# Two expert stages of an audio tower: a bias product over 128 rows, the row copy on ScalarE, products set further apart

## The reference

```python
# first mixture, 8 experts, hidden size 256
h = jax.nn.silu(jnp.einsum('td,edh->eth', xt, w1)) * jnp.einsum('td,edh->eth', xt, w3)
y = jnp.einsum('eth,ehd->etd', h, w2)
out = jnp.einsum('te,etd->td', comb, y) + shared
...
# second mixture, 10 experts, hidden size 512
h = jnp.einsum('nd,edh->enh', x2, e_w1) + e_b1[:, None, :]
h = jax.nn.elu(h)
eo = jnp.einsum('enh,ehd->end', h, e_w2) + e_b2[:, None, :]
y = jnp.einsum('end,ne->nd', eo, gates).reshape(B, T, d)
```

## Time and profile before

| | us |
|---|---|
| median of three runs | 1716.76 |
| lowest and highest | 1712.75, 1718.33 |
| span of the profiled execution | 1722.4 |
| PE busy in that span | 1464.1 (85%) |
| DVE busy | 995.0 (58%) |
| POOL busy | 683.3 (40%) |
| ACT busy | 570.8 (33%) |

### The profile page before, as it was taken

One profiled execution on the slowest core, in us unless ns is written; L12 is line 12 of the kernel. 1 busy time (PEld: TensorE's weight loads), 2 busy tenths in 40 slices (PEclk: granted clock), 3 DMA queues, 4 the chain that ended last, 5 costly groups with the idle time before them and its releaser, 6 DMA issues.

```text
span 1722.4 us, 31035 instructions
## 1 busy us (share of the span) xinstructions
PE 1464.1 (85%) x9288; PEld 1261.0 (73%) x9289; DVE 995.0 (58%) x3333; ACT 570.8 (33%) x1362; POOL 683.3 (40%) x1039
## 2 busy tenths in 40 slices
PE   6679577868888479898999889989999878999985
PEld 3465455648888458687888779877888877999963
DVE  4496776554444565366444744376342627999956
ACT  2434526121222130241134401542033324555524
POOL 0124455345777531225222350235212614556532
PEclk9798798989999776788798969988797989999997
DMA  5003100026777500100010011000000234666634
GB/s 174 1 19 98 19 24 29 20 81 176 219 217 221 171 1 1 37 1 21 17 37 2 1 37 37 1 2 19 19 1 1 78 97 128 176 183 174 182 113 144
DMA packets 102193, 128.32 MB, mean 75 GB/s; under 512 B 21015, under 2 KB 61181, under 8 KB 101842
## 3 DMA queue, kind: packets, MB, share of 16 engines
q1 hardware_dynamic: 88786, 102.36, 20.6%
q0 software_dynamic: 13312, 24.74, 4.4%
HBM read 96.13 MB, written 34.94 MB: 76 GB/s over the span
## 4 chain that ended last, share of the span: by engine, by line
PE 56%; DVE 17%; issue 10%; another core or an unknown queue 5%; DVEq 3%; ACT 3%; POOL 3%; DMA 1%; POOLq 0%; SPq 0%; ACTq 0%
PE psum L970 9%; PE psum L1113 8%; PE psum L979 7%; PE psum L1059 5%; PE psum L962 3%; DVE work L1500 3%; PE psum L1038 3%; PE psum L787 2%; PE psum L1122 2%; PE psum L1008 2%; PE psum L1081 2%; DVE stats L1483 2%; PE psum L1171 2%; PE psum L1092 1%
## 5 line engine op out<-in xcount | busy, mean ns | idle before, releaser
L1113 PE MATMUL psum<-NT,wreg 128*128 128x182 f32 (+1 forms) x1536 | 290.7, 350 | 7.2 <-ACT conv_rows L1401 6.9
L1113 PEld LDWEIGHTS psum<-NT,wreg 128*128 128x128 f32 x1536 | 276.0, 210 | 11.6 <-ACT conv_rows L1401 7.5
L2111 POOL DMA_INDIRECT rows_out<-work,expert_row_kept x208 | 206.2, 991 | 140.1 <-DVE work L1804 115.8
L970 PE MATMUL psum<-work 128*128 128x128 f32 x1664 | 224.2, 278 | 20.2 <-DVE work L1804 18.6
L970 PEld LDWEIGHTS psum<-work 128*128 128x128 f32 x1664 | 208.4, 196 | 27.2 <-issue 16.2
L1309 ACT ACTIVATE work<-psum,work 128x128 f32<-128x128 f32 x416 | 118.3, 368 | 108.7 <-PE psum L970 108.7
L2060 POOL TENSOR_TENSOR rstd<-var_eps,pack 128x6 f32<-128x6 f32 x40 | 56.6, 1417 | 243.2 <-DVE var_eps L1490 243.0
L787 PE MATMUL psum<-pack,work 128*128 128x128 f32 (+1 forms) x336 | 59.8, 335 | 84.1 <-DVE work L1500 74.6
L1831 DVE TENSOR_SCALAR work<-psum,expert_row_kept 128x128 f32<-128x128 f32 x208 | 72.8, 350 | 99.9 <-PE psum L962 42.0
L1822 DVE SCALAR_TENSOR_TENSOR work<-psum,work 128x128 f32<-128x128 f32 x416 | 117.1, 344 | 7.7
L787 PEld LDWEIGHTS psum<-pack,work 128*128 128x128 f32 (+1 forms) x336 | 49.6, 176 | 93.9 <-DVE work L1500 58.7
(11 more groups left out here) (339 smaller groups left out, 2937.6 us busy)
## 6 DMA issues: line engine op xcount, KB each, us to landing
work<-w_and_b SPq DMA_DIRECT2D x104, 258.0 KB
work<-in_ew SPq DMA_DIRECT2D x104, 256.0 KB
work<-rows_in SPq DMA_DIRECT2D x208, 65.0 KB
work<-rows_out SPq DMA_DIRECT2D x32, 384.0 KB, 3.8
rows_out<-work,expert_row_kept POOLq DMA_INDIRECT x208
work<-in_xT SPq DMA_DIRECT2D x8, 375.0 KB, 4.4
w_and_b<-in_ew SPq DMA_DIRECT2D x1, 2560.0 KB
out<-H SPq DMA_DIRECT2D x8, 320.0 KB
```

Of the source, the lines that this page charges most:

```text
L970: r_ = mm(v.ps1[:, c * P:(c + 1) * P], v.w1[:, c * P:(c + 1) * P], v.xT, start=True, stop=True)
L1113: r = mm(bank[:, half * HALF_PAIRS:half * HALF_PAIRS + p1 - p0], weights[:, m * P:(m + 1) * P], product_input(name, g, k, p0, p1), start=( ...
L2111: G.indirect_dma_start(rows_out[m], bass.IndirectOffsetOnAxis(ap=v.dest, axis=0), v.y, None, bounds_check=last, oob_is_err=False).then_inc ...
```

## The change

It has five parts, all in the two expert stages:

1. `ones3` and `rows3` get 128 rows, of which 125 are zero, so that the bias product has 128 rows of weights. DVE sets both to zero at the start of the program.
2. In `experts1` the copy of the transposed rows moves from DVE to ACT, ahead of `exp`. In `experts0` it stays on DVE.
3. `AHEAD` grows: transposition and copy 5 turns ahead (3 before), up-products and `silu`/`exp` 3 (2), `u` 2 (1). `keep` goes from 3 to 2. PE's order in a turn becomes `up`, `xT`, `down`.
4. PSUM banks: up-products 0 to 3, transposition 4 and 5, `down` 6 and 7. `down` of a tile therefore waits for `y` of two tiles before. Semaphores count by tile of the ring (8) instead of by u mod 4.
5. `keep` runs once for two tiles: it waits for both stores of the round before, and copies 4 columns. In `experts0` SP loads the weights anew once `up` has read them (before: once `u` was done).

```diff
-AHEAD = {"xT": 3, "up": 2, "silu": 2, "exp": 2, "u": 1, "down": 0, "y": 0, "keep": 3, "store": 0}
+AHEAD = {"xT": 5, "up": 3, "silu": 3, "exp": 3, "u": 2, "down": 0, "y": 0, "keep": 2, "store": 0}
...
-        ones3 = sb("ones3", [3, P], BF16)
+        ones3 = sb("ones3", [P, P], BF16)
...
-        rows3 = sb("rows3", [3, E1 * P], BF16)
+        rows3 = sb("rows3", [P, E1 * P], BF16)
...
-            v.ps1 = psum[:, 2 * (u % SLOTS), :]
-            v.psx = psum[:, 2 * (u % SLOTS), 0:P]
-            v.psy = psum[:, 2 * (u % SLOTS) + 1, 0:P]
+            v.ps1 = psum[:, u % SLOTS, :]
+            v.psx = psum[:, SLOTS + u % 2, 0:P]
+            v.psy = psum[:, SLOTS + 2 + u % 2, 0:P]
...
-                        sp.wait_ge(pool_done[k], pool.at(phase, "keep", k, r - GROUPS))
+                        sp.wait_ge(pool_done[u // 2], pool.at(phase, "keep", u // 2, i - 1))
                         load_row(u)
-                        sp.wait_ge(dve_done[k], dve.at(phase, "u", k, r - GROUPS))
+                        if m == 0:
+                            sp.wait_ge(pe_done[u], pe.at(phase, "up", u, i - 1))
+                        else:
+                            sp.wait_ge(dve_done[u], dve.at(phase, "u", u, i - 1))
                         load_w1(u)
...
                     e.wait_ge(dve_done[k], dve.at(phase, "u", k, r))
-
+                    if u >= 2:
+                        e.wait_ge(dve_done[u - 2], dve.at(phase, "y", u - 2, i))
+                    else:
+                        e.wait_ge(dve_done[u - 2 + RING], dve.at(phase, "y", u - 2 + RING, i - 1))
...
-                turns(e, [("xT", xT), ("up", up), ("down", down)], begin)
+                turns(e, [("up", up), ("xT", xT), ("down", down)], begin)
...
-                turns(e, [("silu", silu) if m == 0 else ("exp", exp)])
+                def xT(u, i):
+                    v = slots[u]
+                    k, r = u, i
+                    e.wait_ge(pe_done[k], pe.at(phase, "xT", k, r))
+                    nc.scalar.copy(v.xT, v.psx).then_inc(act_done[k], act.step(phase, "xT", k))
+
+                turns(e, [("silu", silu)] if m == 0 else [("xT", xT), ("exp", exp)])
...
-            V.memset(ones3[:], 1.0)
+            V.memset(ones3[:], 0.0)
+            V.memset(rows3[:], 0.0)
+            e.drain()
+            V.memset(ones3[0:3, :], 1.0)
...
-                turns(e, [("xT", xT), ("u", gated if m == 0 else elu), ("y", y)])
+                turns(e, [("xT", xT), ("u", gated), ("y", y)] if m == 0 else [("u", elu), ("y", y)])
...
-                    e.wait_ge(row_stored[u], i * 16 + m * 16 * RITERS)
+                    if u % 2:
+                        return
+                    for x in (u, u + 1):
+                        e.wait_ge(row_stored[x], i * 16 + m * 16 * RITERS)
```

More of the change, by code:

```diff
@@ L93, in run @@
             f(t % RING, i + t // RING)
-    for u in range(-3, 0):
+    for u in range(-FIRST_AHEAD, 0):
         run(0, u, first=True)
@@ L479, in audio_tower @@
         for u, v in enumerate(slots):
-            v.ps1 = psum[:, 2 * (u % SLOTS), :]
-            v.psx = psum[:, 2 * (u % SLOTS), 0:P]
-            v.psy = psum[:, 2 * (u % SLOTS) + 1, 0:P]
+            v.ps1 = psum[:, u % SLOTS, :]
+            v.psx = psum[:, SLOTS + u % 2, 0:P]
+            v.psy = psum[:, SLOTS + 2 + u % 2, 0:P]
         def chunk_steps(names):
             return [f"{n}{c}" for c in range(TILES) for n in names]
-        pe_done = [sem(f"pe_done{k}") for k in range(4)]
+        pe_done = [sem(f"pe_done{k}") for k in range(RING)]
         pe = Steps({
@@ L492, in audio_tower @@
             "shared0": (ITERS, LANES, ["up0_0", "up0_1", "up1_0", "up1_1", "down"]),
-            "experts0": (EITERS, SLOTS, ["xT", "up", "down"]),
+            "experts0": (RITERS, RING, ["xT", "up", "down"]),
             "attention": (ITERS, LANES, ["norm5T", "q0", "q1", "k0", "k1", "v"]
                           + chunk_steps(["sc", "cx"]) + ["oT", "out", "norm6T", "rc1", "scores"]),
-            "experts1": (EITERS, SLOTS, ["xT", "up", "down"]),
+            "experts1": (RITERS, RING, ["xT", "up", "down"]),
             "output": (OUT_ITERS, OUT_LANES, ["z"]),
         })
-        act_done = [sem(f"act_done{k}") for k in range(4)]
+        act_done = [sem(f"act_done{k}") for k in range(RING)]
         act = Steps({
@@ L503, in audio_tower @@
             "shared0": (ITERS, LANES, ["s0_0", "s0_1", "s1_0", "s1_1"]),
-            "experts0": (EITERS, SLOTS, ["silu"]),
+            "experts0": (RITERS, RING, ["silu"]),
             "attention": (ITERS, LANES, ["n5T", "q0", "q1", "k0", "k1", "v"] + chunk_steps(["kt"])
                           + ["oT", "n6T", "rc1", "kept"]),
-            "experts1": (EITERS, SLOTS, ["exp"]),
+            "experts1": (RITERS, RING, ["xT", "exp"]),
             "output": (OUT_ITERS, OUT_LANES, ["norm7"]),
         })
-        dve_done = [sem(f"dve_done{k}") for k in range(4)]
+        dve_done = [sem(f"dve_done{k}") for k in range(RING)]
         dve = Steps({
@@ L524, in audio_tower @@
             "mix_b": (ITERS, (2, 3), ["rstd4"]),
-            "experts0": (EITERS, SLOTS, ["keep"]),
+            "experts0": (RITERS, RING // 2, ["keep"]),
             "attention": (ITERS, LANES, ["rstd5", "b_out", "b_v", "rstd6", "turned"]),
-            "experts1": (EITERS, SLOTS, ["keep"]),
+            "experts1": (RITERS, RING // 2, ["keep"]),
             "output": (OUT_ITERS, OUT_LANES, ["rstd7"]),
@@ L965, in up @@
                     v = slots[u]
[L966 removed]
+                    k, r = u, i
                     e.wait_ge(w1_in[u], i * 16 + (16 + m * 16 * RITERS))
[L968 removed]
+                    if m == 0:
+                        e.wait_ge(dve_done[k], dve.at(phase, "xT", k, r))
+                    else:
+                        e.wait_ge(act_done[k], act.at(phase, "xT", k, r))
                     for c in range(4):
@@ L1826, in y @@
                     v = slots[u]
-                    k, r = slot_round(u, i)
+                    k, r = u, i
                     e.wait_ge(pe_done[k], pe.at(phase, "down", k, r))
                     e.wait_ge(row_stored[u], 16 * i + 16 * RITERS * m)
-                    e.wait_ge(pool_done[k], pool.at(phase, "keep", k, r))
+                    e.wait_ge(pool_done[u // 2], pool.at(phase, "keep", u // 2, i))
                     V.tensor_scalar(v.y, v.psy, v.gate, None, ALU.mult).then_inc(dve_done[k], dve.step(phase, "y", k))
-                turns(e, [("xT", xT), ("u", gated if m == 0 else elu), ("y", y)])
+                turns(e, [("xT", xT), ("u", gated), ("y", y)] if m == 0 else [("u", elu), ("y", y)])
             expert_tiles(0, "experts0")
@@ L2098, in keep @@
                     v = slots[u]
-                    k, r = slot_round(u, i)
-                    e.wait_ge(row_stored[u], i * 16 + m * 16 * RITERS)
+                    if u % 2:
+                        return
+                    for x in (u, u + 1):
+                        e.wait_ge(row_stored[x], i * 16 + m * 16 * RITERS)
                     e.reg_add(last, none, OUT_ROWS - 1)
-                    e.wait_ge(pe_done[k], pe.at(phase, "xT", k, r))
+                    e.wait_ge(pe_done[u + 1], pe.at(phase, "xT", u + 1, i))
                     G.tensor_tensor(keep_seen[:, u:u + 1], w("nought"), w("nought"), ALU.add)
-                    G.tensor_copy(v.kept[:], v.row[:, P:ROW]).then_inc(pool_done[k], pool.step(phase, "keep", k))
+                    pair = work[:, E_AT + u * ROW:E_AT + (u + 2) * ROW].rearrange("p (x c) -> p x c", c=ROW)
+                    G.tensor_copy(kept[:, u:u + 2, :], pair[:, :, P:ROW]
+                                  ).then_inc(pool_done[u // 2], pool.step(phase, "keep", u // 2))
                 def store(u, i):
                     v = slots[u]
-                    k, r = slot_round(u, i)
+                    k, r = u, i
                     e.wait_ge(dve_done[k], dve.at(phase, "y", k, r))
```

35 lines of the change are left out of this document (15 added, 20 removed).

## The result

The changed kernel takes 1713.58 us in the median of 20 runs (1702.02 to 1725.42), the kernel before, run beside it, 1724.65 (1712.04 to 1748.87). The ratio is 0.9943, with a 95% interval of 0.992 to 0.9966: 11 us gained, where 42 were forecast. The profiled execution took 1709.04 us.

The account below looks back on a forecast made before the run. PE was taken to bound the second stage (2.20 per tile, DVE close behind), PE plus waits for late signals the first. From the median 1716.8, 20 and 23 us off and 1 added gave 1675 us, range 1662 to 1698.

Parts of the forecast that it names:

- Second stage: Second expert stage: padding the bias product and moving the row copy to ACT cut 2.20 to 2.01 per tile, gaining 20 us.
- the bias product's load without idle time: Sign expected in the second stage's next profile: no idle time at the padded bias product's weight load, before .12 us.
- that rival: Second stage: the bias product keeps its price, which comes from changing between f32 and bf16; 1695 us, chance .12.
- VectorE's bound: Second stage: DVE needs 2.15 us per tile, close behind PE's 2.20, so a faster PE alone wins .06 at best.
- First stage: First expert stage: larger distances and own banks add .60 of slack against late signals, gaining 23 us (bounds 0 and 31).
- The 22 waits of .97: First stage: PE's waits of `up` for DVE's row copy, 21 us in all, fall to at most .37 each, 8 us.
- the other 10 of the 31 us: First stage: the remaining waiting of PE is short pieces that the .60 of added slack covers.
- Late signals stay in full measure: Rival, first stage: more slack lets POOL run on longer, holds grow, gain 4 us or less; 1694 us, chance .15.
- POOL stays at 1.42 against 1.45: First stage, point for the late-signals rival: POOL's work per tile stays just under PE's turn, leaving almost no pause.
- POOL's backlog shrinks: First stage, point against the late-signals rival: with `keep` paired, POOL needs 1.42 per tile and no longer falls behind PE.
- The cost of eight signals per engine: Ends of both expert stages: each engine passes 12 more waits, costing +1 us in all.
- the slower rival: First stage: row loads with 5 turns of lead come too late; slower by .3% from a 9.2 us landing; chance .05.

Follow-up runs that it names:

- experiment 3: The changed kernel with the bias product back at 3 rows: 1752.12 us, ratio 1.01 to the kernel before; second stage 236.0 us against 211.5.
- pad_only: The kernel before with only the bias product padded to 128 rows: 1629.06 us against 1649.08, ratio .989; second stage 219.6 us.
- experiment 8: The changed kernel with the old distances, in the first stage alone (two variants) or in both stages: ratios .9901, .9941 and .9923 to the kernel before.
- act_stores_c: The changed kernel with first-stage rows stored by ACT's queue as plain DMAs, without POOL's scatter: 1678.47 us against 1725.78 before, ratio .9706; first stage 153.8 us.
- pad_act: The kernel before with the padding and the second stage's row copy on ACT, old distances kept: three runs, ratios .9866, .9823 and .9871 to the kernel before.
- experiment 4: The kernel before and the changed kernel run again unedited: before 1747.47 us (one run); changed 1727.18 and 1715.02 us, ratios .9931 and .992.
- old_dist: The changed kernel with the old distances and PE order in both expert stages: 1724.51 us against 1741.49 for the kernel before, ratio .9923.
- dist0: The changed kernel with old distances in the first stage alone, `up` still ahead of the transposition: 1720.13 us against 1736.19 before, ratio .9901.
- no_pad: The changed kernel with the padding undone, bias product of 3 rows: 1752.12 us against 1736.19 for the kernel before, ratio 1.01.
- after_c: The changed kernel, unedited, run again on another chip: 1715.02 us against 1725.78 for the kernel before, ratio .992; first stage 185.8 us.

## Why the prediction was wrong

**Second stage: right.** Forecast 20 us, measured 21.6 (233.2 to 211.6); PE's turn forecast 2.01, measured 2.00; the bias product's load without idle time, as said. Undoing the padding costs it all (experiment 3). The padded product is still bf16 among f32 products, so the change of type was not its price, and that rival falls. The Trainium skill's rule ("TensorE: Matmul & The Clock Gate", "LDWEIGHTS (loading the stationary operand)") says that the columns of a load and not its rows set its time. That fits the load alone, 90 ns for 3 rows and 100 for 128. It doesn't tell the time of the product: with 3 rows each load stands behind .12 us in which no load runs, and padding alone won 13.6 us (pad_only), where by the rule it would win nothing. The measurement decides.

**VectorE's bound: mis-sized.** "A faster PE alone would win .06 per tile at best" took a turn of 2.15 as VectorE's least. It runs 2.07 when it mainly sets the pace, and the padding alone won 13.6 us, .13 per tile. The sum was not hurt, since the copy moves away.

**First stage: the step that failed.** "The 22 waits of .97 (21 us in all) fall to at most .37" and "the other 10 of the 31 us are short pieces that a .60 covers". Both take the lateness of a signal as given. It isn't: most late signals stay out until POOL pauses, POOL pauses when finished `y` run out, and with more slack it stored four of them in a row where it had stored three. The 9 waits left are 1.47 each and not .37, the new wait of `down` for `y` adds 7 of .6, and the stage took 186.1 us for 184.0 where 161 were forecast (184.0 less 23). This is the first rival, "Late signals stay in full measure", which had a chance of .15: the longest hold grew by 1.0 us, from 2.4 to some 3.4 (experiment 8), by more than the .60 of slack that the sum counts. Its note "POOL stays at 1.42 against 1.45" should have carried more weight than "POOL's backlog shrinks". Its time, 1694, was missed too, by what follows under "the rest". POOL's work per tile did fall, as computed (113.16 us for 99 tiles against 131.01 for 100), and it didn't matter. PE's signals as the thing that is late was read rightly, and act_stores_c shows POOL's scatters behind them on chip III. That the chip decides whether signals come late at all stands nowhere in the prediction; on a chip like V this term would have had little to win: 156.5 us (pad_only) are 1.50 per tile, against PE's 1.45.

**The rest: open.** With 20 us from the second stage and none from the first the ratio would be 1 - 21.6 / 1724.65 = .9875. Three comparisons of the changed kernel gave .992 to .9943, so 8 to 12 us more are missing. pad_act keeps them, with the same stage lengths. Its trace is shorter ahead of and between the expert stages on chip III (391.6 us to the first `up` against 398.9, 837.5 against 856.5 between the stages), but the same kernel differs by as much from chip to chip (837.5 on III, 856.1 on IV for pad_act). A lower granted clock goes with a part of it (experiment 4). What is left of the change beside padding and copy, banks, signals to a slot, paired keeps and distances, costs about that; which of them, and where, no run here tells. The cost of eight signals per engine, forecast at +1, is not seen at the stages' ends. From the last `y` to the end of the last store there are 3.8 and 2.5 us, before 3.1 and 1.8; but old_dist, with eight signals, has 3.3 and 1.8, so what was added there comes with the distances. Late row loads, the slower rival, did not occur: PE's waits in the changed kernel name no row.

## What to carry to other kernels

Before more buffering is bought against late signals, ask what ends the lateness: if it ends when another engine runs out of work, slack feeds that engine and the wait grows with it; what helps is work taken off that engine. A product with few rows among full ones can cost more than twice a full one, so look at the idle time ahead of its weight load. And measure parts of a combined change apart: here two edits gave the whole gain, and beside them the rest took about half of it back (on chip III, where both ran side by side).

## What the runs showed of the hardware that was not expected

- The same kernel differs by 5.7% between chips (1647.05 and 1741.49 us for the kernel before). Some 30 us of it lie in the first expert stage: 156.5 and 157.4 (pad_only, pad_act) against 184.0 to 196.1 with the same first stage. In that stage PE's signals come 14 ns after their record on chips V and VI whatever POOL does, on I to IV up to 3.47 us.
- The late signals aren't confined to that stage. Between the expert stages, where POOL also issues rows of indirect DMAs, every trace of chips I to IV has 18 to 28 signals over .3 us late, the latest by 5.9 to 9.2 us, and that stretch takes 837.5 to 868.1 us; no trace of V or VI has one, and it takes 784.1 to 821.4.
- In the second expert stage no trace has a signal over .3 us late. POOL issues one indirect DMA per tile there too, but with more time from one's end to the next one's start: in the changed kernel 1.00 us in the median and over .79 in nine of ten cases, where the first stage has .51 in the median.
- In the first stage none was late where POOL issued no indirect DMA, even on such a chip (act_stores_c), and none from 420 to 575 in dist0, where POOL paused in nearly each turn.
- A 3-row product among 128-row ones costs .24 us more than one padded to 128 (no_pad: 236.0 less 211.5, over 104 tiles), though it does less.
- Runs of one kernel differ with the mean granted clock (between its levels of 1.2 and 2.4 GHz): 1.0 us for .001 in the 20 runs of the changed kernel, with a correlation of -.76. Between the expert stages the longer stretch also has the lower clock, here pad_only on chip V and after_c on chip III, though the late signals of III are in it too.

```profile
543.00:1327.00 784.00, 711.37 (x4386) 634.83 (x4386) 412.05 (x1183) 245.37 (x527) 255.58 (x263) 0.86 0.09 28
```

```profile
584.00:1441.00 857.00, 753.28 (x4386) 675.66 (x4386) 412.99 (x1183) 244.21 (x529) 252.91 (x261) 0.83 0.08 26
```
